# Moving half of the next step's level sums ahead of the mixing products, and the row transposes ahead of the B/C work, in a chunked scan

## Chip, cores, metric

One core of a Trainium2 chip runs the whole kernel in one launch. The metric is the device time of one execution in microseconds; the kernel before has a median of 4289.28 us in three runs (4289.17 to 4289.45).

## The reference, cut to what matters

The program is a small network on 2 sequences of 2048 tokens with 128 channels, float32: a block A (selective scan, time crystal, wavelet attention, mixture of experts, each behind a layer norm and a mask), then a top-4-head attention with 64 channels per head, an attention B, and the first attention once more. The change lies in the selective scan of block A alone:

```python
xz = x @ w_in                       # x: layer-normed tokens
xc, z = xz[..., :d_inner], xz[..., d_inner:]
xc = silu(causal_dwconv(xc, conv_w))
Bt, Ct = split(xc @ w_bc)
dt = softplus(xc * w_dt + dt_bias)
# per token t, channel c, state n
h   = exp(dt_t * A)[..., None] * h + (dt_t * xc_t)[..., None] * B_t[:, None, :]
y_t = einsum('bcn,bn->bc', h, C_t)
out = (y + d_skip * xc) * silu(z) @ w_out
```

## The kernel before

The scan (`phase_M`) takes 32 steps of 64 tokens of both sequences at once: 64 tokens of sequence 0 in partitions 0 to 63, those of sequence 1 in 64 to 127, 256 inner channels along the free axis. Within a step the recurrence is solved by levels: for distances of 1, 2, 4 and so on, decays are exponentials of partial sums of dt times A.

Each engine has its own function that lists its work in order (`pe`, `act`, `dve`, `pool`); signals (semaphores) tie them together, and an engine waits in that order. Of step i these matter:

- TensorE (`pe`): `pe_mix(i)` (L593, L595, L597), the mixing products, which wait for the weighed values of step i, its masked pairs, and y of step i-1. Then `pe_front(i + 1, j)`, j = 0 to 3 (L546 in steps 0 to 3, L549 later): the partial sums of the next step, four groups; with `pe_turn(i + 2)` (L557) between j = 1 and j = 2. Then `pe_bc(i + 2)` (L565, L569), `pe_y(i - 1)` (L604), `pe_pairs(i + 2)` (L577), in even steps `pe_out` (L613), then every eighth step `pe_t_ln` (L504) and `pe_t_out` (L515, L516, tanh products), and at the end the convolution of step i + 8 (`pe_conv`, L527 and L530), in step 0 four of them, in step 2 three, in step 1 and from step 24 on none. Before the convolutions 8, 16 and 24 (in steps 2, 8 and 16) stands `pe_ln` (L496), which turns the layer-normed rows of the next 512 tokens of each sequence into channels.
- ScalarE (`act`): the exponentials of the sums (`act_front`, L957 and L959), copies of `pe_turn` (L965), `pe_bc` (L972) and `pe_y` (L978); in the first step of each group of four absolute value and exponential of the new step sizes (`act_exps`, L940, L942), in the second the logarithm (`act_log`, L946); then `act_ln` (L902), the copies of the turned rows, where there are any, and the gate activation of the convolution (`act_silu`, L936), which writes m_xz. Every eighth step it has the root (L908) and the normed tokens of the time crystal (L916), or those of the scan (L896).
- VectorE (`dve`): `dve_skip`, `dve_mix` (L751 to L761, ending with y), `dve_raw` (L708, L709) for the convolution of the step before, then in the second step of a group `dve_rest` (L717, L719), in the third `dve_step_size` (L723, L724, L726), the masked pairs (L731), and the output.
- GpSimd (`pool`): `pool_front(i + 1)`, the weighing of the decays (L1076, three operations) and the skip product (L1080); then `pool_split(i + 2)` (L1062 to L1065), which cuts dt times A into three bfloat16 parts for `pe_front`, or, in the third step of a group, `pool_scale` (L1052, a split, L1055), which waits for `dve_step_size`.

PSUM banks 2 and 3 form a ring: the sums, the convolutions, the turned rows and the tanh products take them in turn, in a fixed list. Each use waits until the one two places ahead of it has been read by ScalarE:

```python
def pe_ring(*use):
    n = ring_at[use]
    if n >= 2:
        T.wait_ge(*ring_read[ring[n - 2][0]](*ring[n - 2][1:]))
    return ring_bank(*use)
```

The list has, per step i: the four sums of step i + 1, then tln or tc if any, then ln if any, then the convolution. `ring_read` is the exponential for a sum, and the gate activation for a convolution. Besides, `pe_front(i, 0)` waits for the split of step i from step 4 on.

Of the kernel before, what the change touches and what calls it, by code (L numbers as in the profile page):

```python
# [99 lines left out]
def build(nc, a, out, shape, phases=("M", "C", "D", "E", "F", "E2")):  # L100
# [5 lines left out]
    with ctx:  # L106
# [162 lines left out]
        def phase_M():  # L269
# [13 lines left out]
            with ExitStack() as st:  # L283
# [206 lines left out]
                def pe_ln(g):  # L490

                    T.wait_ge(*normed(g))
                    for b in bs:
                        bk = pe_ring("ln", g, b)
                        for q in range(4):
                            last = T.transpose(bank(bk)[:, q * P:(q + 1) * P], norm[:, 8 * (g % 2) + 4 * b + q, :], ident[:, :])  # L496
                        last.then_inc(*ln_turned.up(g, b))
# [54 lines left out]
                def pe_turn(i):  # L552
                    if i < Q4:
                        T.wait_ge(*silued(i))
                    bk = pe_misc("turn", i)
                    for c in range(C2):
                        last = T.transpose(bk[:, c * P:(c + 1) * P], xz[:, i % SLOTS, c * P:(c + 1) * P], ident[:, :])  # L557
                    last.then_inc(*x_turned.up(i))
# [22 lines left out]
                def pe_mix(i):  # L581

                    s, r = i % 2, i % 3
                    T.wait_ge(*val_done(i, 2))
                    T.wait_ge(*gm_done(i))
                    T.wait_ge(*state_done(-1))
                    if i:
                        T.wait_ge(*y_done(i - 1))
                    at = lambda b: dict(start=True, stop=True, skip_group_check=True, tile_position=(W * b, W * b))
                    slot = lambda l, b: bank(4 + l // 2)[half(b), (l % 2) * DI:(l % 2 + 1) * DI]  # L590
                    for l in range(LV):
                        for b in bs:
                            T.matmul(slot(l, b), gm[half(b), r, l, :], val[half(b), s, l, :], **at(b))  # L593
                    for b in bs:
                        T.matmul(slot(LV, b), bcs[half(b), r, 3 * N:4 * N], state[half(b), :], **at(b))  # L595
                    for b in bs:
                        last = T.matmul(slot(LV + 1, b), bcs[half(b), r, 0:N], val[half(b), s, SUF, :], **at(b))  # L597
                    last.then_inc(*mixed.up(i))
# [30 lines left out]
                def pe():  # L629
                    pe_ln(0)  # L630
                    T.wait_ge(*ld.all())
                    T.wait_ge(*tapped(0))
                    for k in range(Q4):
                        pe_conv(k)
                    for i in range(2):
                        pe_turn(i)
                        pe_bc(i)
                        pe_pairs(i)
                    pe_pool(0)
                    for j in range(4):  # L640
                        pe_front(0, j)
                    for i in ks:
                        pe_mix(i)
                        for j in range(4):
                            if i + 1 < SK:
                                pe_front(i + 1, j)
                            if j == 1 and i + 2 < SK:
                                pe_turn(i + 2)
                        if i + 2 < SK:
                            pe_bc(i + 2)  # L650
                        if i:
                            pe_y(i - 1)
                        if i + 2 < SK:
                            pe_pairs(i + 2)
                        if i == 0:
                            pe_pool(1)
                        if i == 1:
                            for b in bs:
                                pe_router(b)
                        if i % 2 == 0 and i:  # L660
                            pe_out(i // 2 - 1)
                        if i >= 10 and i % SLOTS == 2:
                            pe_t_ln(i // SLOTS - 1)
                        if i >= 10 and i % SLOTS == 3:
                            pe_t_out(i // SLOTS - 1)
                        for k in convs.get(i, ()):
                            if k % SLOTS == 0:
                                pe_ln(k // SLOTS)
                            pe_conv(k)
                    pe_y(SK - 1)  # L670
                    pe_out(NT - 1)
                    pe_t_ln(NG - 1)
                    pe_t_out(NG - 1)
                    leave(T)
# [224 lines left out]
                def act_ln(g):  # L899
                    for b in bs:  # L900
                        A.wait_ge(*ln_turned(g, b))
                        A.activation(chan(b, g), bank(ring_bank("ln", g, b)), ACT.Identity, bias=gain[:, 1:2],  # L902
                                     scale=gain[:, 0:1]).then_inc(*chan_done.up(g, b))
# [57 lines left out]
                def act_turn(i):  # L961
                    A.wait_ge(*x_turned(i))
                    if i >= 2:
                        A.wait_ge(*bc_made(i - 2))
                    A.copy(xT[:, i % 2], misc_bank("turn", i)[:, 0:C2 * P].rearrange("p (c t) -> p c t", c=C2)).then_inc(*xT_done.up(i))  # L965
# [19 lines left out]
                def act():  # L985
                    act_std("H", h_rs, 0)
                    act_std("M", n_rs, 0)
                    A.wait_ge(*ld.all())
                    act_ln(0)
                    act_std("H", h_rs, 1)  # L990
                    for k in range(Q4):
                        act_silu(k)
                    A.activation(neg_a[:, :], neg_a[:, :], ACT.Exp).then_inc(*exp_a.up(0))
                    act_exps(0)
                    for i in range(2):
                        act_turn(i)
                        act_bc(i)
                    act_log(0)
                    for j in range(4):
                        act_front(0, j)  # L1000
                    for i in ks:
                        q, at = i // Q4 + 1, i % Q4
                        for j in range(4):
                            if i + 1 < SK:
                                act_front(i + 1, j)
                            if j == 1 and i + 2 < SK:
                                act_turn(i + 2)
                        if i + 2 < SK:
                            act_bc(i + 2)
                        if i:  # L1010
                            act_y(i - 1)
                        if i == 1:
                            act_router()
                        if at == 0 and i and q < NQ:
                            act_exps(q)
                        if at == 1 and q < NQ:
                            act_log(q)
                        if i == 1 or (i % SLOTS == SLOTS - 1 and i // SLOTS + 2 < NG):
                            act_normed(i // SLOTS + (1 if i == 1 else 2))
                        if i >= 10 and i % SLOTS == 2:  # L1020
                            act_t_ln(i // SLOTS - 1)
                        if i >= 10 and i % SLOTS == 3:
                            act_tanh(i // SLOTS - 1)
                        for k in convs.get(i, ()):
                            if k % SLOTS == 0:
                                act_ln(k // SLOTS)
                            act_silu(k)
                        if i == 3:
                            A.wait_ge(*angle(0))
                            A.activation(cs[:, 0:1], tau[:, :], ACT.Sin)  # L1030
                            A.activation(cs[:, 1:2], th[:, :], ACT.Sin).then_inc(*sines.up(0))
                        if i >= 8 and i % SLOTS == 0:
                            act_t_std(i // SLOTS - 1)
                        if i >= 9 and i % SLOTS == 1:
                            act_t_normed(i // SLOTS - 1)
                        if i == 0:
                            act_std("M", n_rs, 1)
                            act_exps(1)
                    act_y(SK - 1)
                    act_t_std(NG - 1)  # L1040
                    act_t_normed(NG - 1)
                    act_t_ln(NG - 1)
                    act_tanh(NG - 1)
                    leave(A)
# [2103 lines left out]
```

## Time and profile before

| | |
|---|---|
| median of three runs | 4289.28 us |
| profiled execution | 4288.47 us |
| its span | 4287.2 us, 74987 instructions |
| TensorE busy (matmul) | 3584.7 us, 84% |
| VectorE busy | 3288.7 us, 77% |
| ScalarE busy | 2847.2 us, 66% |
| GpSimd busy | 1082.8 us, 25% |
| mean granted clock of TensorE | 0.827 |

The page cuts the span into 40 slices of 107 us; the scan's steps lie in the first five. The later slices belong to the other blocks. In the rows below, times are microseconds from the start of the span, a second number is a duration, and what stands in brackets at the end is how long the engine sat idle ahead of the instruction and what released it.

### The profile page before, as it was taken

The numbers are of one execution on the slowest core, as the hardware profiler recorded it, in microseconds if no ns is written. First come the engines' busy times: TensorE is split into PE (matmuls) and PEld (weight loads), VectorE is DVE, ScalarE is ACT, GpSimd is POOL, SyncE is SP. The second block draws the span as 40 slices with busy tenths as digits, with TensorE's granted clock in tenths as the row PEclk, the third lists the DMA queues.
The fourth block names the chain that finished last, engine by engine and source line by source line (L and its number), as shares of the span: only waits on it lengthen the run. The fifth ranks groups of instructions, "written<-read, shape, count | busy, mean of one in ns | idle before, by whom it ended". The sixth has DMA issues, their size and how long they took to land.

```text
span 4287.2 us, 74987 instructions
## 1 busy us (share of the span) xinstructions
PE 3584.7 (84%) x29132; PEld 1881.5 (44%) x29132; DVE 3288.7 (77%) x5099; ACT 2847.2 (66%) x4856; POOL 1082.8 (25%) x1610
## 2 busy tenths in 40 slices
PE   6888769998999998999998666666666668899999
PEld 4656512222444445676665122222122215566766
DVE  6888678886301137787888999999999987778887
ACT  3666426655434444666667999999999995566665
POOL 2666632100667630000000233322322210000000
PEclk8999859998999998999998555555555559999999
DMA  1000043320422110000000111011111010000000
GB/s 49 1 1 1 1 74 56 63 40 11 118 41 40 21 24 6 14 5 12 2 9 11 22 23 23 18 20 23 23 23 22 18 23 16 7 12 7 17 2 12
DMA packets 256883, 97.53 MB, mean 23 GB/s; under 512 B 223861, under 2 KB 241922, under 8 KB 256514
## 3 DMA queue, kind: packets, MB, share of 16 engines
q1 hardware_dynamic: 256530, 92.74, 10.9%
q8 instruction: 232, 3.80, 0.4%
q14 instruction: 121, 0.99, 0.1%
HBM read 31.75 MB, written 2.23 MB: 8 GB/s over the span
## 4 chain that ended last, share of the span: by engine, by line
PE 46%; DVE 32%; issue 12%; ACT 7%; POOL 1%; DMA 1%; SPq 1%; DVEq 0%; ACTq 0%; POOLq 0%
DVE d_negmax L2990 14%; PE psum L2540 7%; PE psum L2569 7%; DVE f_m_E L2645 6%; PE psum L2555 6%; PE psum L2223 5%; PE psum L2245 5%; ACT d_junk L3045 3%; PE psum L1501 2%; PE psum L1489 2%; DVE wl_negmax L1625 2%; DVE f_pT_E L2664 2%; PE psum L1478 2%; PE psum L593 1%; PE psum L527 1%
## 5 line engine op out<-in xcount | busy, mean ns | idle before, releaser
L2990 DVE TENSOR_REDUCE d_negmax<-psum 128x1 f32<-128x1024 f32 x1024 | 1170.8, 1210 | 8.5 <-PE psum L2930 6.4
L3045 ACT ACTIVATE d_junk<-psum,d_negmax 128x1024 bf16<-128x1024 f32 x1024 | 1136.8, 1127 | 29.7 <-DVE d_negmax L2990 25.3
L2930 PE MATMUL psum<-f_k,f_q_swapped 64*128 64x512 bf16 x2048 | 622.1, 604 | 420.0 <-ACT d_junk L3045 416.1
L2741 ACT ACTIVATE hidden<-psum,f_nm_E 128x1024 f32<-128x1024 f32 x512 | 566.5, 1113 | 146.6 <-DVE f_nm_E L2648 146.4
L2645 DVE TENSOR_REDUCE f_m_E<-psum 128x1 f32<-128x1024 f32 x512 | 601.9, 1216 | 50.8 <-PE psum L2540 49.5
L2540 PE MATMUL psum<-f_k,f_q_swapped 64*128 64x512 f32 x1024 | 527.3, 625 | 6.6 <-ACT hidden L2741 6.6
L2540 PE MATMUL psum<-f_k,f_q 64*128 64x512 f32 x1024 | 527.1, 625 | 2.9 <-DVE f_v_E L2636 1.9
L2748 ACT COPY f_pT_E<-psum 128x512 f32<-128x512 f32 x512 | 299.9, 586 | 321.2 <-PE psum L2555 321.2
L2569 PE MATMUL psum<-f_pT_E,f_v_E 128*64 128x128 f32 x8192 | 505.5, 276 | 2.5 <-DVE residual L2675 2.5
L2664 DVE COPY f_pT_E<-psum 128x512 f32<-128x512 f32 x512 | 351.3, 686 | 163.3 <-PE psum L2555 153.6
L2930 PEld LDWEIGHTS psum<-f_k,f_q_swapped 64*128 64x128 bf16 x2048 | 107.8, 101 | 830.4 <-ACT d_junk L3045 762.2
L2569 PEld LDWEIGHTS psum<-f_pT_E,f_v_E 128*64 128x64 f32 x8192 | 444.1, 137 | 20.0 <-ACT f_pT_E L2748 2.8
L2555 PEld LDWEIGHTS psum<-ident,hidden 64*128 64x128 f32 x8192 | 317.5, 140 | 242.9 <-issue 194.7
L2555 PE MATMUL psum<-ident,hidden 64*128 64x64 f32 x8192 | 358.5, 227 | 54.9 <-DVE f_pT_E L2664 50.8
L2357 POOL TENSOR_TENSOR moe_h<-moe_h,moe_gates_on_all 128x512 f32<-128x512 f32 x256 | 322.4, 1293 | 322.3 <-DMA moe_gates_on_all<-moe_gate_spill 188.9
L1766 ACT ACTIVATE wl_p<-psum 128x1024 f32<-128x1024 f32 x256 | 255.3, 1023 | 212.5 <-PE psum L1489 211.7
L1625 DVE TENSOR_REDUCE wl_negmax<-psum 128x1 f32<-128x1024 f32 x256 | 305.2, 1220 | 69.1 <-PE psum L1478 65.6
L2335 ACT ACTIVATE moe_h<-psum,moe_b 128x512 f32<-128x512 f32 x256 | 174.9, 688 | 254.7 <-PE psum L2245 254.7
L2223 PE MATMUL psum<-moe_h,moe_w 128*128 128x512 f32 x512 | 232.3, 597 | 3.4 <-POOL moe_h L2357 3.4
L3045 ACT ACTIVATION_READ_ACCUMULATOR d_junk<-psum,d_negmax 128x1 f32 x1024 | 214.9, 210 | 0.0
L2245 PE MATMUL psum<-normed_channels,moe_w 128*128 128x512 f32 x448 | 203.5, 597 | 4.3 <-DMA moe_w<-in_moe_w 4.3
L2540 PEld LDWEIGHTS psum<-f_k,f_q 64*128 64x128 f32 x1024 | 161.3, 189 | 92.6 <-ACT hidden L2741 78.4
(352 smaller groups left out, 4730.2 us busy)
## 6 DMA issues: line engine op xcount, KB each, us to landing
moe_gates_on_all<-moe_gate_spill SPq DMA_DIRECT2D x16, 1024.0 KB, 11.8
f_q_swapped<-f_q SPq DMA_DIRECT2D x64, 128.0 KB, 2.4
moe_w<-in_moe_w SPq DMA_DIRECT2D x15, 256.0 KB, 6.2
residual<-in_hidden_states SPq DMA_DIRECT2D x2, 768.0 KB, 7.9
out<-residual SPq DMA_DIRECT2D x1, 1024.0 KB, 7.3
wl_qT<-wl_q_rows SPq DMA_TRANSPOSE x48, 3.4
residual<-in_hidden_states SPq DMA_DIRECT2D x2, 256.0 KB, 3.2
m_taps<-in_m_conv SPq DMA_DIRECT2D x4, 128.0 KB
```

The costliest lines, as they stand in the source:

```text
L1625: V.tensor_reduce(negm[:, i, h:h + 1], two(slot("max", b, h, i)), X, ALU.max, negate=True).then_inc(*maxed.up(b, h, i))
L2223: last = T.matmul(acc, w2[:, e * FT + f, :], hbuf[:, n % 2, f, :], start=False, stop=(e == E_ - 1 and f == FT - 1))
L2245: T.matmul(bank(f), w1(e)[:, f * P:(f + 1) * P], chans[:, b, PAD + g * BANK:PAD + (g + 1) * BANK], start=True, stop=True).then_inc(*made.u ...
L2540: last = T.matmul(bank(2 * f + jj), (q if jj == h else q_sw)[half, w, qs], k2[half, w, h, f, :], start=True, stop=True)
L2555: last = T.transpose(bank(4 + r)[:, q * 64:(q + 1) * 64], pb[half, u % 2, kt * P:(kt + 1) * P], ident[half, half])
L2569: last = T.matmul(bank(6)[64 * h:64 * h + 64, 0:P], vt[:, n % 2, kt, h, :], pT[:, (2 * t + h) % 4, kt, :], start=(kt == 0), stop=(kt == NT ...
L2645: last = V.tensor_reduce(m2[:, u % 4, f:f + 1], two(2 * f), X, ALU.max)
L2664: V.tensor_copy(pT[:, u % 4, 8 * g:8 * g + 8, 64:P], bank(5).rearrange("p (q n) -> p q n", n=64)).then_inc(*pT_dve.up(u, g))
L2741: A.activation(pb[:, u % 2, f * 2 * BANK:(f + 1) * 2 * BANK], two(2 * f), ACT.Exp, bias=nm[:, u % 4:u % 4 + 1], scale=SC, accum_out=rs[:, ...
L2930: last = T.matmul(bank(2 + 2 * (at % 3) + jj), kT[half, s, jb * P:(jb + 1) * P], qT[half, s, hf * BANK:(hf + 1) * BANK], start=True, stop= ...
L2990: V.tensor_reduce(mh[:, t % 2, n // 2, n % 2:n % 2 + 1], two(2 + 2 * (at % 3)), X, ALU.max, negate=True).then_inc(*maxed.up(at))
L3045: A.activation(junk[:, at % 3, :], two(2 + 2 * (at % 3)), ACT.Exp, bias=mh[:, t % 2, n // 2, n % 2:n % 2 + 1], accum_out=sh[:, t % 2, n // ...
```

## The change

On TensorE, in steps i where i + 1 isn't a multiple of four (24 of the 31 steps that have a next one), `pe_front(i + 1, 0)` and `pe_front(i + 1, 1)` are issued ahead of `pe_mix(i)`; the others stay behind it. `pe_ln` moves from directly ahead of the convolution to directly behind the fronts, ahead of `pe_bc`. On ScalarE `act_ln` moves likewise, ahead of `act_bc`, and so ahead of `act_y` and `act_exps`. The ring's list stays as it is; so do all instructions of VectorE and GpSimd.

```diff
                     for i in ks:
+                        ahead = 2 if i + 1 < SK and (i + 1) % Q4 else 0
+                        for j in range(ahead):
+                            pe_front(i + 1, j)
                         pe_mix(i)
                         for j in range(4):
-                            if i + 1 < SK:
+                            if i + 1 < SK and j >= ahead:
                                 pe_front(i + 1, j)
                             if j == 1 and i + 2 < SK:
                                 pe_turn(i + 2)
+                        for k in convs.get(i, ()):
+                            if k % SLOTS == 0:
+                                pe_ln(k // SLOTS)
                         if i + 2 < SK:
                             pe_bc(i + 2)
...
                         for k in convs.get(i, ()):
-                            if k % SLOTS == 0:
-                                pe_ln(k // SLOTS)
                             pe_conv(k)
...
+                        for k in convs.get(i, ()):
+                            if k % SLOTS == 0:
+                                act_ln(k // SLOTS)
                         if i + 2 < SK:
                             act_bc(i + 2)
...
                         for k in convs.get(i, ()):
-                            if k % SLOTS == 0:
-                                act_ln(k // SLOTS)
                             act_silu(k)
```

## Rows read from the trace of the kernel before

**Rows 1.** Waits of TensorE, 57 to 517 us: total, times, longest.

```profile
PE psum L549 <- ACT m_decay L959: 19.3, 27, 4.3
PE psum L527 <- ACT normed_channels L902: 8.6, 3, 3.7
PE psum L549 <- ACT m_xz L936: 5.0, 5, 1.2
```

**Rows 2.** Timeline of TensorE, steps 3 to 7: start, duration, instruction, idle ahead.

```profile
128.71 1.48 PE L549 MATMUL psum<-m_dta_parts,level_sums_bf 128*128 128x256 bf16 x12
...
136.31 2.81 PE L593 MATMUL psum<-m_val,m_pairs 64*64 64x256 f32 x24
...
148.66 2.81 PE L593 MATMUL psum<-m_val,m_pairs 64*64 64x256 f32 x24
...
159.86 2.81 PE L593 MATMUL psum<-m_val,m_pairs 64*64 64x256 f32 x24
...
163.46 0.83 PE L549 MATMUL psum<-m_dta_parts,level_sums_bf 128*128 128x256 bf16 x6
165.14 0.83 PE L549 MATMUL psum<-m_dta_parts,level_sums_bf 128*128 128x256 bf16 x6 [0.85 <-ACT m_xz L936]
165.81 0.38 PE L557 MATMUL psum<-ident,m_xz 128*128 128x128 f32 x2
...
179.67 1.47 PE L549 MATMUL psum<-m_dta_parts,level_sums_bf 128*128 128x256 bf16 x12 [1.71 <-POOL m_dta_parts L1065]
```

**Rows 3.** Timeline of VectorE, steps 4 and 6, and line 723 (ns min/median/max).

```profile
140.32 1.23 DVE L751 TENSOR_TENSOR m_z<-psum,m_decay 128x1024 f32<-128x1024 f32 x1
...
146.49 0.83 DVE L709 TENSOR_TENSOR m_dtx<-m_dtx,m_dtb 128x256 f32<-128x256 f32 x1
...
164.07 1.22 DVE L751 TENSOR_TENSOR m_z<-psum,m_decay 128x1024 f32<-128x1024 f32 x1
...
172.19 1.75 DVE L723 TENSOR_TENSOR m_one_plus<-m_one_plus,m_dta 128x1024 f32<-128x1024 f32 x1
...
L723 DVE TENSOR_TENSOR m_one_plus<-m_one_plus,m_dta x8: 1226/2229/2840, 52.4 to 455.9; 128x1024 f32<-128x1024 f32 x8
```

**Rows 4.** Timeline of ScalarE, steps 4 and 5.

```profile
147.36 1.06 ACT L940 ACTIVATE m_dta<-m_dtx 128x1024 f32<-128x1024 f32 x1 [2.21 <-DVE m_dtx L709]
...
150.82 0.60 ACT L936 ACTIVATE m_xz<-psum 128x512 f32<-128x512 f32 x1
...
162.12 1.06 ACT L946 ACTIVATE m_one_plus<-m_one_plus 128x1024 f32<-128x1024 f32 x1 [3.32 <-DVE m_dta L719]
163.20 1.28 ACT L936 ACT_TABLE_LOAD   x1
164.49 0.60 ACT L936 ACTIVATE m_xz<-psum 128x512 f32<-128x512 f32 x1
```

**Rows 5.** Timeline of GpSimd, step 3: weighing of step 4, end of split 5.

```profile
130.70 4.28 POOL L1076 TENSOR_TENSOR m_val<-m_decay,m_dtx 128x768 f32<-128x768 f32 x3 [6.43 <-issue]
...
137.82 0.73 POOL L1065 TENSOR_TENSOR m_dta_parts<-m_dta_rest,m_dta_parts 128x256 bf16<-128x256 f32 x1
```

**Rows 6.** Timeline of TensorE: sums of step 20, mixings 20 and 31, sums of step 24.

```profile
359.83 1.48 PE L549 MATMUL psum<-m_dta_parts,level_sums_bf 128*128 128x256 bf16 x12
...
372.03 2.81 PE L593 MATMUL psum<-m_val,m_pairs 64*64 64x256 f32 x24
...
415.57 1.48 PE L549 MATMUL psum<-m_dta_parts,level_sums_bf 128*128 128x256 bf16 x12
...
506.53 2.81 PE L593 MATMUL psum<-m_val,m_pairs 64*64 64x256 f32 x24 [0.80 <-POOL m_val L1076]
```

**Rows 7.** Stretches of TensorE: length, busy (instructions), granted clock, DMA share, GB/s.

```profile
201.90:205.70 3.80, 3.77 (x20) 0.60 0.00 0
...
316.00:319.80 3.80, 0.11 (x3) 0.86 0.00 0
319.80:324.30 4.50, 4.50 (x22) 0.50 0.00 0
324.30:328.50 4.20, 4.20 (x34) 0.85 0.01 4
```

## Prediction

> **What bounds the kernel now.** I first read the page's slices: the scan (phase M) fills only the first 0.52 ms of 4287 us, and the change touches nothing outside it. Then I read who TensorE waits for inside the scan [rows 1]: 19.3 us in 27 waits of the sum products (L549) for the exponentials (L959), 8.6 us in three waits of the convolution products for the turned rows (L902), and 5.0 us in five waits for the gate activation m_xz (L936). These waits are what the change goes for. Then I followed steps 4 to 8 engine by engine. Names for the rest: E(i) is the end of the mixing products of step i, f0 to f3 of a step are its four sum groups (pe_front, j = 0 to 3), k is the convolution that a step issues last.
>
> TensorE carries most steps: the mixings of steps 4, 5 and 6 start at 136.31, 148.66 and 159.86 [rows 2], 12.35 and 11.20 us apart, and it waits little between. Mixing 6 runs 3.60 us (159.86 to 163.46). Beside that chain runs a second one, through three engines. After mixing 4 VectorE combines (L751, 140.32), weighs the newest tokens (L709, ends 147.32) [rows 3]; only then can ScalarE do its absolute value and exponential (L940, 147.36, after 2.21 us of waiting), load a table and run the gate activation of convolution 12 (150.82 to 151.42) [rows 4]. In step 5 it is the same with the logarithm: L946 waits 3.32 us, starts at 162.12, and activation 13 ends at 165.09 [rows 4]. In the kernel before, mixing 5 (148.66) and mixing 6 (159.86) are long under way when these activations end. That is the cover which I look at.
>
> **The change, part by part.** It removes and adds no operation. Part one moves f0 and f1 of step i+1 ahead of mixing i for 24 of the 31 steps that have a next one. Part two moves the row transposes (three times in the scan) and their copies ahead of the B/C work.
>
> *What f0 and f1 bring with them: two waits.* f0 waits for the three-part split of step i+1 by GpSimd. f1 waits for the bank that it writes: banks 2 and 3 alternate, a step uses five turns (four sums, one convolution), so f1 of step i+1 takes the bank of the convolution issued at the end of step i-1, and has to wait until ScalarE's gate activation has read it. The trace has this wait: f1 of step 7 starts at 165.14, 0.85 us idle, released by m_xz L936 [rows 2]; f0 had started at 163.46. Today mixing 6 stands ahead of that wait. After the change mixing 6 stands behind it, and behind mixing 6 the whole VectorE chain. TensorE doesn't pass a waiting product: in that row the transposes behind it (165.81) need nothing from ScalarE, and waited too.
>
> So in the first two steps of each group of four a loop closes: mixing i, combine, new tokens, exps or logarithm, gate activation, f1, mixing i+1. I add it from rows.
> - First step of a group: E(4) = 136.31 + 3.60 = 139.91, activation 12 ends at 151.42: 11.5 us. Plus 0.05 for the release, 0.66 for f1 (half of the 1.32 that twelve sum products take to the next start), 3.60 for the mixing: 15.8. VectorE began 0.4 us late there (140.32) [rows 3], so I take 15.6.
> - Second step: E(5) = 152.26, activation 13 ends at 165.09: 12.8, plus 4.3 is 17.1. GpSimd works less beside VectorE in a longer step, so 16.9.
> - Third step: f0 of the next group (step 8) starts at 179.67, after a wait for the split [rows 2]; VectorE had started mixing 6 at 164.07 [rows 3]: 15.6. VectorE's L723 took 1.75 us there; its fastest is 1.226 and its median 2.229 [rows 3], and the fast ones come where GpSimd is idle. In the new order GpSimd has finished its weighing by the time VectorE comes to L723, so I take 14.0 (13.3 to 15.6).
> - Last step: the next group's first f0 isn't moved. From f0 of step 4 (128.71) to the end of split 5 (137.82 + 0.73 = 138.55) it is 9.8 us [rows 2, 5]; then f0, f1 and the mixing, 1.32 + 3.60 + 0.05: 14.8. Mixing 4 itself needed nothing of split 5 and started at 136.31; its move behind f0 costs 2.3 us at once.
>
> A group is then 14.8 + 15.6 + 16.9 + 14.0 = 61.3 us. In two of five groups the tanh products stand in between: f0 of step 20 to mixing 20 is 12.2 us [rows 6], so the first term is 17.2, 2.4 more. Five groups: 306.5 + 4.8 = 311.3. Before, from f0 of step 4 (128.71) to f0 of step 24 (415.57), it was 286.9 [rows 2, 6]. **Plus 24.4 us.**
>
> *The clock.* Ten of these steps leave TensorE waiting for 3.3 to 6 us right ahead of f1 and the mixing (in step 4 its other work ends some 8 us after E(4), the release comes at 11.5). After 3.8 us of near idleness at 316.0 the granted clock was 0.50 for 4.5 us and 0.85 for the next 4.2; after the one ending at 201.9 it was 0.60 for 3.8 us, and then full but for a little [rows 7]. So the first lost 2.9 us, the second 1.6. f1 and mixing are only 4.3 us of work, so I take 1.6 for each: **plus 16 us** (0 to 28). The shorter waits ahead of f0 (2.3 us) I leave at nothing: after 1.71 us at 179.67 the products ran at full pace [rows 2].
> The Trainium skill's page "TensorE: Matmul & The Clock Gate", Part 1, says that the array's clock is halved after an idle stretch and comes back after sustained work; the trace agrees at 316.0 to 324.3. By it none of the ten waits would be free.
>
> *Table loads.* ScalarE's load stands inside both loops; it took 1.28 us at 163.20, and the activation followed 0.01 us behind it at 164.49 [rows 4].
> The Trainium skill, "ScalarE: Activation LUTs", section "What ACT_TABLE_LOAD costs", adds a drain of about 1.38 us to each switch. By that ten loops would be 14 us longer in all; the trace shows no such gap, and the measurement decides.
>
> *Steps 24 to 31* have no convolution, so f1 finds its bank free. What closes here: mixing i, f2 of step i+1, exponential, last weighing, skip product, split, f0, f1, mixing i+1. From the durations of step 4 (its weighing 4.28 us in three operations, 9.8 us from f0 to split) I estimate 11 to 12 us a step, 14 where ScalarE also has the layer norm's root. Eight mixings, the last ending at 506.53 + 3.60 = 510.1, took 94.6 us from 415.57 [rows 6]; I estimate 101. **Plus 6 us** (-1 to +12).
>
> *Part two and the saved waits.* In the old order the early rows would save two waits of 3.7 us and one of 1.2 [rows 1], and the half clock behind the two, 12 to 14 us. In the new order the convolution is no longer what is late there: its activation waits on ScalarE for the exps anyway. The 0.2 us that f2 waits for the exponential in a plain step goes too, but lies inside a step whose length is now set elsewhere. I credit 1 us, in step 2, whose mixing follows no such loop. Steps 0 to 3 otherwise even out.
>
> Sum: 24.4 + 16 + 6 - 1 = 45.4, taken as 45.5. The profiled execution took 4288.5 us, 0.8 under the median of 4289.3; with it 4334, against the median 4335.
>
> **The rivals.**
> 1. *The loops close, but the clock holds.* For it: waits of 1.7 us left the clock alone. Against it: both waits near 3.8 us didn't. With the low ends of the other terms (third step 13.3, steps 24 to 31 at -1) 4308, with the middle ones 4319.
> 2. *The saved waits win* (faster). Mechanism: the three early turnings and 24 saved waits of f2 (some 0.33 us each, 8 us) stay on the path, 20 us together: 4269. It needs the gate activation to be read before f0 has run, 0.7 us behind the convolution; it decides in steps 4, 5, 8, 9 and so on. The rows say that it is read 2.8 us (step 4: 151.42 against 148.66) and 5.2 us (165.09 against 159.86) after the convolution's end. In its favour is only that rows 1 show the waits it removes.
> 3. *They cancel*: the loops cost only the direct delay of each mixing, without carrying on into the next step, about half of 24, and part two returns 12: within 8 us of today.
> 4. *Worse*: half clock through the whole of each f1 and mixing and contended VectorE everywhere (group 63.4): 4360 and over.
>
> **How the numbers follow.** Forecast 0.60 (4319 to 4360); rival 1 0.20; rival 4 0.05; rival 3 0.08; rival 2 0.07. A measurement of this kernel tells about 0.2% (8.6 us) from no change. Slower by more: 0.85; within: 0.08; faster: 0.07. The range from 4308 (rival 1, low ends) to 4360 leaves out rivals 2, 3 and 4.
>
> **What would show it.** In the profile after: waits of L549 for m_xz L936 grow from 5.0 us to 35 us or more, ten of them over 3 us; mixings of steps 4, 5 and 6 lie 15.5 to 19 us apart; waits of the convolution for L902 vanish; f2's waits for L959 almost vanish; the scan ends some 45 us later, everything after it keeps its length. Wrong if mixings stay 11 to 12 us apart, or if waits for m_xz are few.

## The result

The kernel after takes 4332.81 us, the median of three runs (4328.47 to 4336.06), against 4289.28 us before: 1.0099 times as long, with a 95% interval of 1.0081 to 1.0117. It is slower by 43.5 us; the forecast was 4335, in a range of 4319 to 4360. The profiled execution took 4328.47 us, 40.0 more than that of before.

From the page of after: the span, the busy times that answer to the table of before, and two rows of its 40 slices (108 us each) in tenths, TensorE's busy share and its granted clock:

```profile
span 4327.2 us, 74987 instructions
...
PE 3598.8 (83%) x29132; PEld 1886.0 (44%) x29132; DVE 3262.2 (75%) x5099; ACT 2852.5 (66%) x4856; POOL 1062.1 (25%) x1610
...
PE   6888859999899998999998666666666659899999
...
PEclk8999968999999999999999555555555559899999
```

As many instructions as before. TensorE is busy 14 us longer and VectorE 26 us shorter, while the span is 40 us longer. So neither engine got much more work; what grew is idle time.

The waits of TensorE in the scan, in the order total, times, longest, from 57 to 570 us (line numbers after the change lie 3 to 5 higher: L936 is now L940, L1065 is L1070, L959 is L963):

```profile
PE psum L549 <- ACT m_xz L940: 35.0, 11, 4.7
PE psum L549 <- POOL m_dta_parts L1070: 34.4, 19, 5.0
...
PE psum L549 <- ACT m_decay L963: 1.1, 5, 0.2
```

Against [rows 1]: the waits that the change goes for are gone. Those of the sums for the exponentials fell from 19.3 to 1.1 us, and none of the convolution for the turned rows is left. In their place stand 35.0 us for the gate activation, which were 5.0, and 34.4 us in 19 for GpSimd's split, which were 6.1 in 4.

Steps 4 to 7 after, on TensorE (start, duration, instruction, idle time ahead and its releaser):

```profile
127.44 1.48 PE L549 MATMUL psum<-m_dta_parts,level_sums_bf 128*128 128x256 bf16 x12
...
137.42 1.47 PE L549 MATMUL psum<-m_dta_parts,level_sums_bf 128*128 128x256 bf16 x12 [2.31 <-POOL m_dta_parts L1070]
138.82 2.81 PE L593 MATMUL psum<-m_val,m_pairs 64*64 64x256 f32 x24
...
153.38 1.33 PE L549 MATMUL psum<-m_dta_parts,level_sums_bf 128*128 128x256 bf16 x6 [3.02 <-ACT m_xz L940]
154.64 3.94 PE L593 MATMUL psum<-m_val,m_pairs 64*64 64x256 f32 x24
...
171.09 1.46 PE L549 MATMUL psum<-m_dta_parts,level_sums_bf 128*128 128x256 bf16 x6 [4.70 <-ACT m_xz L940]
172.48 3.55 PE L593 MATMUL psum<-m_val,m_pairs 64*64 64x256 f32 x24
...
190.22 1.90 PE L549 MATMUL psum<-m_dta_parts,level_sums_bf 128*128 128x256 bf16 x12 [2.62 <-POOL m_dta_parts L1070]
```

and on ScalarE and VectorE, for [rows 3, 4]:

```profile
149.26 1.06 ACT L944 ACTIVATE m_dta<-m_dtx 128x1024 f32<-128x1024 f32 x1 [3.25 <-DVE m_dtx L713]
...
152.72 0.60 ACT L940 ACTIVATE m_xz<-psum 128x512 f32<-128x512 f32 x1
...
159.56 1.23 DVE L755 TENSOR_TENSOR m_z<-psum,m_decay 128x1024 f32<-128x1024 f32 x1 [7.57 <-PE psum L597]
...
168.07 1.06 ACT L950 ACTIVATE m_one_plus<-m_one_plus 128x1024 f32<-128x1024 f32 x1 [3.81 <-DVE m_dta L723]
...
170.44 0.60 ACT L940 ACTIVATE m_xz<-psum 128x512 f32<-128x512 f32 x1
...
177.02 1.23 DVE L755 TENSOR_TENSOR m_z<-psum,m_decay 128x1024 f32<-128x1024 f32 x1 [7.52 <-PE psum L597]
```

In before mixings 4, 5 and 6 lay 12.35 and 11.20 us apart [rows 2]; here mixings 5 and 6 lie 17.8 us apart. Read the rows in a circle. The gate activation ends at 153.32; f1 starts at 153.38, and mixing 5 behind it at 154.64. Its last product lets VectorE go at 159.56, after 7.57 us without work. VectorE's work lets ScalarE take the logarithm at 168.07, the activation behind it ends at 171.04, and f1 starts at 171.09. So the circle is f1, mixing, VectorE, ScalarE, f1, and every engine in it waits for the one before it. VectorE's waits for the mixing's last product grew from 66.1 us in 18 to 143.1 us in 24 (57 to 570 us).

For the runs below I take one mark as the scan's end, the transposes of its last y, here before and after:

```profile
515.91 0.69 PE L604 MATMUL psum<-ident,m_y 128*128 128x128 f32 x2 [5.34 <-DVE m_y L761]
```

```profile
562.79 0.69 PE L604 MATMUL psum<-ident,m_y 128*128 128x128 f32 x2 [5.33 <-DVE m_y L765]
```

The scan is longer by 46.9 us.

### The profile page after: what moved, and what is told of

The parts are those of the page before. It is cut to its first block, busy times and chain, and to the rows that moved or that the text cites. A ratio compares the mean times of both kernels' runs of the same rounds, so it can differ in the third digit from the quotient of the medians.

```text
span 4327.2 us, 74987 instructions
## 1 busy us (share of the span) xinstructions
PE 3598.8 (83%) x29132; PEld 1886.0 (44%) x29132; DVE 3262.2 (75%) x5099; ACT 2852.5 (66%) x4856; POOL 1062.1 (25%) x1610
## 3 DMA queue, kind: packets, MB, share of 16 engines
q1 hardware_dynamic: 256530, 92.74, 10.7%
## 4 chain that ended last, share of the span: by engine, by line
PE 40%; DVE 29%; issue 12%; ACT 6%; DMA 1%; SPq 0%; POOL 0%; DVEq 0%; ACTq 0%; POOLq 0%
DVE d_negmax L2995 14%; PE psum L2545 7%; PE psum L2574 6%; DVE f_m_E L2650 6%; PE psum L2560 6%; PE psum L2228 5%; PE psum L2250 5%; ACT d_junk L3050 3%; PE psum L1506 2%; PE psum L1494 2%; DVE wl_negmax L1630 2%; DVE f_pT_E L2669 2%; PE psum L1483 2%; ACT wl_p L1771 1%; DVE residual L2680 1%
```

## The experiments

All diffs are against the kernel after. "Scan end" is the start of the product just shown. Before ran beside them at 4288.3 to 4290.3 us.

| kernel | scan end | median us | to before [95%] |
|---|---|---|---|
| before | 515.9 | 4289.28 | |
| after | 562.8 | 4332.81 | 1.0099 [1.0081, 1.0117] |
| ln_only | 509.2 | 4276.76 | 0.9967 [0.9954, 0.9979] |
| fronts_only | 581.5 | 4349.01 | 1.0132 [1.0115, 1.0149] |
| one_ahead | 530.5 | 4302.77 | 1.0027 [1.0016, 1.0038] |
| silu_first | 530.9 | 4301.31 | 1.0027 [1.0017, 1.0036] |
| split_first | 552.2 | 4328.62 | 1.0099 [1.0082, 1.0116] |
| both_first | 519.8 | 4294.03 | 1.0010 [1.0001, 1.0020] |
| both_none_ahead | 508.2 | 4276.66 | 0.9977 [0.9968, 0.9987] |
| fill | 573.7 | 4348.95 | 1.0147 [1.0130, 1.0164] |
| fill_half | 549.5 | 4322.70 | 1.0079 [1.0062, 1.0096] |
| only_0 | 522.9 | 4291.50 | 1.0009 [1.0000, 1.0019] |
| only_1 | 526.5 | 4295.34 | 1.0016 [1.0006, 1.0026] |
| only_2 | 533.2 | 4308.22 | 1.0046 [1.0029, 1.0063] |

### The two parts apart

ln_only is part two alone, one line of TensorE's list:

```diff
-                        ahead = 2 if i + 1 < SK and (i + 1) % Q4 else 0
+                        ahead = 0
```

> Part two alone: the turned rows go early, no sum group goes ahead of the mixing. The last y transpose of the scan starts at 515.9 us before and at 562.8 after the change. Theory (the loop through the gate activation costs the time, part two is sound by itself): the waits of 3.7, 3.7 and 1.2 us for L902 go, and with them the half clock behind two of them, so the scan ends 10 to 14 us before 515.9, and the kernel takes 4275 to 4279. Rival (part two harms too, because the copies now stand ahead of those of B/C and y on ScalarE): 4289 or more.

It is the fastest kernel of the study together with both_none_ahead below: 4276.76 us (4275.96 to 4279.37), 12.5 under before. The scan ends at 509.2, 6.8 earlier and not 10 to 14. Its two long waits did go. Ahead of the convolution of step 8 stood 3.69 us for the copies; mixing 8 to mixing 9 was 187.25 to 205.73 in before and is 186.17 to 199.87 now, 18.5 against 13.7 us. The second such place gives 5.4 us. Three of these ten microseconds are lost again at step 11 (mixing 11 to 12 took 15.8 us, now 18.8), by the clock. The granted clock over 243.2 to 250.3 is 0.52 (stretch: length, busy, clock, DMA share, GB/s), where the same products in before, the second row, had 1.00:

```profile
243.20:250.30 7.10, 7.10 (x31) 0.52 0.00 0
```

```profile
249.50:253.58 4.08, 4.08 (x30) 1.00 0.00 0
```

By the medians the kernel gains 5.7 us more than its scan, by the two profiled executions 2.3 us more (4288.47 against 4279.37). Where it gains them was not found; the last section comes back to it.

fronts_only is part one alone: `pe_ln` and `act_ln` back where they were in before.

```diff
-                        for k in convs.get(i, ()):
-                            if k % SLOTS == 0:
-                                pe_ln(k // SLOTS)
                         if i + 2 < SK:
                             pe_bc(i + 2)
...
                         for k in convs.get(i, ()):
+                            if k % SLOTS == 0:
+                                pe_ln(k // SLOTS)
                             pe_conv(k)
```

> Part one alone: two sum groups ahead of the mixing, the rows turned late as before. Theory: in steps 8 and 16 the copies of the turned rows now wait behind the exps on ScalarE, the convolution behind the copies and its gate activation behind that, all inside the loop that ends in f1; so this is 7 to 9 us longer than the whole change, scan end near 571, kernel near 4341. Rival (the convolution is off the path in the new order, part two worth nothing): scan end 562 to 564.

The sign is as expected, the size isn't: the scan ends at 581.5, so part two is worth 18.7 us inside the new order, not about 8.

```profile
PE psum L549 <- ACT m_xz L939: 33.0, 10, 4.7
PE psum L549 <- POOL m_dta_parts L1068: 32.0, 19, 5.7
...
PE psum L527 <- ACT normed_channels L905: 10.7, 3, 4.7
```

(L939, L1068 and L905 stand here for L940, L1070 and L906 of after.)

The three waits of the convolution are back, and are longer (10.7 us). In this order they cost more than their own length: the convolution's activation is what f1 of the next step but one waits for, so a late convolution delays the next mixing too. From mixing 8 to mixing 9 and from 16 to 17 it took 20.4 and 20.5 us, against 15.3 in the kernel after. That makes 10.3 of the 18.7 us; 3.9 us more are there by mixing 8 (206.40 against 202.55), and the rest was not placed.

### Which of the moved groups

one_ahead moves f0 only. f1, which needs the convolution's bank, stays behind the mixing.

```diff
-                        ahead = 2 if i + 1 < SK and (i + 1) % Q4 else 0
+                        ahead = 1 if i + 1 < SK and (i + 1) % Q4 else 0
```

> The whole change, but only f0 goes ahead of the mixing. f0 waits only for the split and for a bank whose reader is long done; f1, the group with the wait for the gate activation, stays behind. Theory: the ten waits of L549 for m_xz ahead of a mixing vanish, mixings of steps 4 to 7 lie 11 to 13 us apart again, scan end 505 to 518, kernel within 12 us of before. Rival (any sum group ahead of the mixing does it, through the split and the lower clock): scan end above 540.

Between the two: 530.5. All waits for m_xz are gone, and 32 of the 47 us with them, so the bank is the main cause. But it leaves 14.6 us over before, and more than 21 over ln_only. They sit at the other signal:

```profile
PE psum L549 <- POOL m_dta_parts L1070: 45.3, 18, 4.1
```

f0 waits for a split that GpSimd finishes only after weighing, and now a mixing waits behind f0. My forecast priced it in the first step of each group, at the first f0 of the next group, and in steps 24 to 31. Here it also stands ahead of mixings 6, 10, 14, 18 and 22, 3.19 us each time.

### The two late producers

silu_first takes the cause away at ScalarE: the gate activation is issued ahead of the exponential, the logarithm and the normed tokens, none of which the convolution needs. (`act_t_ln` and `act_tanh` of the time crystal, which stood right ahead of it, move up with it; the lines below don't show them.)

```diff
-                        if at == 0 and i and q < NQ:
-                            act_exps(q)
-                        if at == 1 and q < NQ:
-                            act_log(q)
...
                         for k in convs.get(i, ()):
                             act_silu(k)
+                        if at == 0 and i and q < NQ:
+                            act_exps(q)
+                        if at == 1 and q < NQ:
+                            act_log(q)
```

> The whole change, and ScalarE does the gate activation ahead of exps and logarithm (and of the normed rows) instead of behind them. Nothing else differs. Theory: the bank of the convolution is read 0.7 us after its end, so f1 waits under 0.5 us; the loop is broken; mixings 11 to 13.5 us apart, scan end 505 to 525. What is left are the waits for the split. Rival (the loop closes through the exponential or the split anyway): scan end above 545.

530.9: 32 of 47 us come back, as with one_ahead, by another way. The activation of step 4 now starts at 149.44, right behind the convolution, and f0, f1 and mixing 5 follow one another at full pace:

```profile
149.33 1.59 PE L549 MATMUL psum<-m_dta_parts,level_sums_bf 128*128 128x256 bf16 x12
150.85 2.81 PE L593 MATMUL psum<-m_val,m_pairs 64*64 64x256 f32 x24
```

Mixing 5 starts at 150.85 and mixing 6 at 163.30, 12.5 us apart, where the kernel after has 17.8. What is left is the split:

```profile
PE psum L549 <- POOL m_dta_parts L1070: 40.7, 19, 5.0
```

split_first takes that away instead: GpSimd splits step i+2 ahead of weighing step i+1.

```diff
                     for i in ks:
+                        if i + 2 < SK and i % Q4 != 2 and i + 2 > Q4:
+                            pool_split(i + 2)
                         if i + 1 < SK:
                             pool_front(i + 1)
                         if i % Q4 == 2 and i // Q4 + 1 < NQ:
                             pool_scale(i // Q4 + 1)
-                        elif i + 2 < SK and i % Q4 != 2 and i + 2 > Q4:
-                            pool_split(i + 2)
```

> The whole change, and GpSimd splits step i+2 ahead of weighing step i+1 instead of behind it; ScalarE's order as in the change. The scan's last y transpose starts at 562.8 us after the change, 530.9 with the gate activation first, 509.2 with part two alone. Theory: of the 34 us that f0 waits for the split most go, but in the groups up to step 23 they lie beside the loop through the gate activation except in the first step of a group and steps 24 to 31, so the scan ends 10 to 18 us earlier, at 545 to 553, and the waits of f1 for m_xz stay at 35 us or rise. Rival (the split's waits are the main cost): scan end below 535.

552.2, as expected. The split waits fall from 34.4 to 10.3 us, and the waits for m_xz grow from 35.0 to 39.3: while the circle through ScalarE is closed, an earlier f0 mostly waits longer at f1.

```profile
PE psum L549 <- ACT m_xz L940: 39.3, 12, 4.7
PE psum L549 <- POOL m_dta_parts L1070: 10.3, 5, 2.6
```

both_first has both edits.

> The whole change with both: gate activation ahead of exps and logarithm, split ahead of the weighing. Theory: both waits that came with the change are gone, scan end 503 to 515, kernel 4275 to 4287. Rival (something else in the new order costs, as VectorE starting its combination later): scan end above 522.

519.8, outside the 503 to 515 that I gave. All but freed of both producers (4.8 us in 3 are left for m_xz, 8.9 in 5 for the split), the early sums still don't pay. The sums f2 wait again for the exponentials, 19.3 us in 14, as much as in before, and the waits of the mixing for the last y are 8.4 us in 2, where after had 2.3 in 1:

```profile
PE psum L549 <- ACT m_decay L963: 19.3, 14, 3.6
PE psum L549 <- POOL m_dta_parts L1070: 8.9, 5, 2.6
PE psum L593 <- DVE m_y L765: 8.4, 2, 6.1
```

both_none_ahead tells what the order of sums and mixing is worth once both producers are early: it is both_first with `ahead = 0`.

> Part two, gate activation first and split first, but no sum group ahead of the mixing. It tells what the early sums bring once their waits are gone. Theory: scan end 500 to 509, the gate activation's waits of L549 (5.0 us) gone; the early sums are worth 5 us at most either way. Rival (early sums pay once freed): both_first ends its scan over 6 us before this one.

508.2, as expected, and 4276.66 us (4268.98 to 4285.65 in ten runs). The early sums cost 11.6 us of the scan even here. Of these, 2.9 us are there by mixing 4 (138.08 against 135.22), nearly nothing is added up to mixing 12 (251.06 against 247.95), and 3.8 us come behind mixing 24 (420.17 against 412.39). What costs them was not tested. Against ln_only the two freed producers bring 1.0 us of the scan and nothing in the time (0.9977 and 0.9967, intervals overlapping). They are worth something only where sums go early.

### The clock

The stretch behind the wait of step 5, f1 and mixing 5 of the kernel after, had a granted clock of 0.67, and that behind the wait of step 6 had 0.71:

```profile
153.38:158.60 5.22, 5.22 (x32) 0.67 0.02 3
...
171.09:176.10 5.01, 5.01 (x34) 0.71 0.01 3
```

fill puts products into ten of the waits ahead of f1: those of the mixing once more, into the banks that the mixing overwrites next. They need nothing that is new and nobody reads them. The first try took too many of them, 12 to 38.

```diff
+                fill = {5: 24, 6: 38, 9: 12, 10: 32, 13: 24, 14: 38, 17: 12, 18: 32, 21: 24, 22: 38}
...
                         for j in range(ahead):
+                            if j == 1 and i in fill:
+                                pe_fill(i, fill[i])
                             pe_front(i + 1, j)
```

> The whole change, with extra products between f0 and f1 in the ten steps where f1 waits for the gate activation: 12 to 38 of the mixing's own products, about as long as the wait (1.3 to 4.2 us), written where the mixing writes right after. TensorE then isn't idle there. Theory (idleness ahead of f1 costs half clock in f1 and the mixing, 14 us by the longer durations in the trace): the L593 groups of steps 5, 6, 10, 13, 14, 18, 21, 22 go from 3.5 to 5.1 us back to 2.8, and the scan ends 8 to 14 us earlier, at 549 to 555. Rival (the clock isn't on the path): scan end 560 to 565.

The filling of step 5 took 5.40 us for a wait of 3.02, so the mixing came later by more than the clock gave back: 573.7. It is no measure of the clock's price; it shows only that the mixings are back at 2.81 us.

```profile
150.92 5.40 PE L609 MATMUL psum<-m_val,m_pairs 64*64 64x256 f32 x48
...
157.01 2.81 PE L593 MATMUL psum<-m_val,m_pairs 64*64 64x256 f32 x24
```

fill_half has about half as many, 4 to 18 products (each is two instructions in the trace; `fill = {5: 12, 6: 18, 9: 4, 10: 14, 13: 12, 14: 18, 17: 4, 18: 14, 21: 12, 22: 18}`).

> As fill, with about half as many extra products (4 to 18 products, two array instructions each), since in fill they ran 5.4 us where f1 waited 3.0, and held f1 back. Now they should end just before the gate activation. Theory (half clock in f1 and the mixing is on the path): mixings of steps 5, 6, 10, 13, 14, 18, 21, 22 take 2.8 us in the L593 group, f1 0.8, and the scan's last y transpose starts at 548 to 555, against 562.8 after the change. Rival (clock not on the path): 560 to 565.

This one fits: in step 5 the filling leaves 0.29 us of waiting, and all waits for m_xz together are 5.7 us.

```profile
150.19 2.81 PE L609 MATMUL psum<-m_val,m_pairs 64*64 64x256 f32 x24
...
153.28 0.83 PE L549 MATMUL psum<-m_dta_parts,level_sums_bf 128*128 128x256 bf16 x6 [0.29 <-ACT m_xz L956]
154.04 2.81 PE L593 MATMUL psum<-m_val,m_pairs 64*64 64x256 f32 x24
```

```profile
153.28:157.60 4.32, 4.32 (x38) 1.00 0.00 0
```

With more work on TensorE the scan ends at 549.5, 13.3 us earlier than after. In one place, mixing 5, it is 154.64 + 3.94 against 154.04 + 2.81, 1.7 us. But not all of the 13.3 us lies behind the ten waits. From mixing 4 to 7, 8 to 11, 12 to 15, 16 to 19 and 20 to 23, where the fillings stand, fill_half gains 3.0, 1.9, 2.9, 1.3 and 3.2 us, 12.3 together. Between mixings 11 and 12, where none stands, it gains 3.5 (21.63 us in after, 18.15 here), because after ran the last tanh products and the convolution there at a clock of 0.60 (262.0 to 270.5), and this kernel at 1.00 (255.9 to 262.0). And behind mixing 24 it loses 2.5 again, with mixings 30 and 31 at 5.38 and 4.50 us. So the clock behind the ten waits costs some 12 us. It isn't the same for each: in after, seven of the ten waits are followed by a mixing of 3.55 to 5.05 us, and three, of 1.68, 3.03 and 1.69 us, by one of 2.81. Two waits of the same length differ (steps 13 and 21):

```profile
285.09 0.83 PE L549 MATMUL psum<-m_dta_parts,level_sums_bf 128*128 128x256 bf16 x6 [3.03 <-ACT m_xz L940]
285.85 2.81 PE L593 MATMUL psum<-m_val,m_pairs 64*64 64x256 f32 x24
...
412.31 0.88 PE L549 MATMUL psum<-m_dta_parts,level_sums_bf 128*128 128x256 bf16 x6 [3.02 <-ACT m_xz L940]
413.12 4.40 PE L593 MATMUL psum<-m_val,m_pairs 64*64 64x256 f32 x24
```

### Which step of the group

only_0, only_1 and only_2 move f0 and f1 in one of the three steps of each group alone (i % 4 = 0, 1, 2):

```diff
-                        ahead = 2 if i + 1 < SK and (i + 1) % Q4 else 0
+                        ahead = 2 if i + 1 < SK and i % Q4 == 0 else 0
```

> Part two, and f0 and f1 ahead of the mixing only in the first step of each group of four (8 steps), where the early group waits for the split, and not for exps or logarithm. Base is part two alone, scan end 509.2. Theory: steps 4, 8, 16 and 24 lose the split's 2.3 us and some clock, scan end 517 to 524. Rival (early sums are harmless here): 507 to 512.

> The same, only in the second step of each group: mixings 5, 9, 13, 17, 21 now stand behind the gate activation that follows the exps. Theory: each loses 3 to 4 us and some clock, what follows doesn't loop, scan end 524 to 534. Rival (one step alone is absorbed by the slack of the next): 509 to 515.

> The same, only in the third step of each group: mixings 6, 10, 14, 18, 22 stand behind the gate activation that follows the logarithm, and VectorE's step sizes for the next group behind that mixing. Theory: VectorE starts 5 to 7 us later in these steps, of which 1 to 2 us is slack in the split of the next group; scan end 529 to 540. Rival (absorbed): 509 to 515. The three together should make up the 53.6 us between part two alone and the whole change.

All three fall in their ranges: 522.9, 526.5 and 533.2. Over ln_only (509.2) that is 13.7, 17.3 and 24.0 us, in sum 55.0, and all together cost 53.6. The costs add up, but this doesn't show that the steps leave each other alone, for the waits are not those of the kernel after. ln_only has 7.1 us in 6 for the split and 5.0 in 5 for m_xz. With i % 4 = 0 f0 waits 17.0 us in 9 for the split; with 1 f1 waits 11.4 us in 10 for m_xz, and f0 13.7 in 8 for the split. The dearest, 2, falls in its range by another wait than I named: for m_xz it waits 4.5 us in 5, less than ln_only, and for the split 40.0:

```profile
PE psum L549 <- POOL m_dta_parts L1070: 40.0, 14, 5.8
```

## Why the prediction was right

The likeliest case came, near the middle of its range. By its own steps:

- **The circle through ScalarE.** Foretold were 35 us or more of waits for m_xz, ten of them over 3 us, and mixings of steps 4 to 6 lying 15.5 to 19 us apart. There are 35.0 us in 11, eight of them over 3 us, and the mixings start at 138.82, 154.64 and 172.48, 15.8 and 17.8 us apart. silu_first, which takes this cause away at ScalarE, and one_ahead, which takes only f1 out of it, end within 0.4 us of each other, 32 us earlier than after. That is shown.
- **A group's length.** From f0 of step 4 to f0 of step 24 I had 311.3 + 16 = 327.3 us; it is 127.44 to 449.39, 322.0. The third step was 13.2 us and not 14.0 (VectorE's start at 177.02 to f0 at 190.22, and 13.2 in the four other groups too): 4 us over five groups. The lower end that I had given was 13.3. VectorE's L723 [rows 3], L727 now, shows it: in its seven later instances the median was 2.29 us and is 1.22, which had been the fastest. That it's GpSimd, done earlier, which leaves VectorE its pace fits with this (in before it worked beside L723 at 227.86, which took 2.84 us; in after it stands idle from 180.59 to 185.82, around L727 at 183.26), but was not tested apart. Before and after (ns, min/median/max):

```profile
L723 DVE TENSOR_TENSOR m_one_plus<-m_one_plus,m_dta x7: 1536/2285/2840, 113.9 to 455.9; 128x1024 f32<-128x1024 f32 x7
```

```profile
L727 DVE TENSOR_TENSOR m_one_plus<-m_one_plus,m_dta x7: 1215/1220/1682, 115.2 to 499.3; 128x1024 f32<-128x1024 f32 x7
```

- **The clock.** 16 us forecast for ten waits, some 12 measured by fill_half in the steps that it fills. Rival 1, that it holds, falls: 0.67 and 0.71 were granted. But the prediction's "none of the ten waits would be free" is not so: they were 1.68 to 4.70 us long and not 3.3 to 6, and three were free. That the waits of 2.3 us at f0 cost nothing held in step 4 (1.47 us at 137.42), not everywhere: at 190.22, after 2.62 us, the products took 1.90.
- **Steps 24 to 31.** The term that was mis-sized: +6 us (-1 to +12) forecast; from f0 of step 24 to the scan's mark it was 100.3 us (415.57 to 515.91) and is 113.4 (449.39 to 562.79), +13.1. I had put the circle at 11 to 12 us a step, and from mixing 24 (460.88) to mixing 31 (551.74) it is 13.0 on average. Part of it is clock, which I hadn't counted here: f0 waits up to 5.01 us, and the stretch from that wait on had a clock of 0.66.

```profile
486.03 2.72 PE L549 MATMUL psum<-m_dta_parts,level_sums_bf 128*128 128x256 bf16 x12 [5.01 <-POOL m_dta_parts L1070]
488.68 4.17 PE L593 MATMUL psum<-m_val,m_pairs 64*64 64x256 f32 x24
```

```profile
486.00:494.00 8.00, 7.97 (x47) 0.66 0.00 0
```

  Four mixings of these steps run over 2.81 us (3.44, 4.17, 3.17, 4.28), 3.8 us in all, and three pairs of f0 and f1 over 1.48 (2.47, 2.72, 2.72), 3.5 us. Before has slow ones there too (a mixing of 4.43 us in step 26, 1.6 us), so in these products the clock makes some 5.7 us of the 13.1. The other products were not added up.
- **Part two.** 1 us credited, and f0 of step 4 does start 1.3 us earlier (127.44 against 128.71); against fronts_only part two is worth 18.7. I had said that the convolution isn't what is late in the new order. It is, in the steps where it waits for the turned rows. The sum isn't touched by it, since I took the steps with the turned rows as plain ones. On its own I had given it 12 to 14 us in the old order, and it measured 6.8.
- **The split.** The signs that I gave name only m_xz, and the split's waits are as long, 34.4 us in 19. In the sum they were not forgotten: 5.9 us stand ahead of mixings 4, 8 and 16, 10.3 at the first f0 of a group, 15.1 in steps 24 to 31, and for each of these the sum has a term. Only 3.1 us stand ahead of mixings 6, 10, 14, 18 and 22, where f1 behind them waits longer for m_xz. What the split costs is 10.6 us of the 47 by split_first, and 11 with the circle open (530.9 against 519.8).
- **Rival 2** (the saved waits win) asked for activations read at once. both_first comes near that, and still ends 11.6 us behind the same kernel with the sums in their old place. The waits for exponentials that this rival saves are not saved there: they are 19.3 us again.

The errors (5 us too much in the groups, 7 too little behind them) cancel: 46.9 us of scan measured, 45.5 forecast. That the sum comes so near is in part luck; the mechanism isn't. The time itself rose by less, 40.0 us between the profiled executions, since later stages gave some back. One place of it: in the attention of block A, behind a wait of 2.37 us that both kernels have (ahead of 1009.20 and of 1055.85), before ran at a clock of 0.61 over 1011.0 to 1024.8, and after at 1.00 in the same products:

```profile
1011.07 1.90 PE L1501 MATMUL psum<-wl_p,wl_v 128*9 128x512 f32 x8
...
1024.78 1.05 PE L1501 MATMUL psum<-wl_p,wl_v 128*9 128x512 f32 x8
```

```profile
1056.85 1.05 PE L1506 MATMUL psum<-wl_p,wl_v 128*9 128x512 f32 x8
...
1066.15 1.05 PE L1506 MATMUL psum<-wl_p,wl_v 128*9 128x512 f32 x8
```

These are the first and the fifth of the same groups of products. Between them the offset of the two kernels shrinks from 45.8 us (1056.85 - 1011.07) to 41.4 (1066.15 - 1024.78). The other 2.5 us were not placed.

## What to carry to other kernels

An engine works through its list in order, so moving work ahead of a critical instruction moves that work's waits ahead of it too. List what the moved work waits for, a bank taken in turns included, and see when each signal comes; if one of them hangs on the instruction that was passed, the move closes a circle. The length of a wait in the list isn't what its removal brings: 18 us of waits for exponentials went with the change and longer ones came in their place, while one move of three row transposes (ln_only), for 8.6 us of waits, took 12.5 us off the kernel.

## What the runs showed of the hardware

- The clock of a stage far behind the edit differs between the traces of two kernels: 0.61 in before and 1.00 in after, some 500 us behind the scan. Whether the edit did it isn't shown, for one and the same kernel, before, ran between 4281.2 and 4295.9 us over nineteen runs. ln_only gained 12.5 us in time for 6.8 us in the scan. Between kernels whose scans differ by less than some 5 us this is more than the difference; the scan's mark tells them apart better than the time does. Whether the clock makes all of that scatter wasn't tested.
- A clock dip needs no long wait directly in front of it: ln_only had 0.52 over 7.1 busy microseconds (243.2 to 250.3), where before had none in the same products, and in the 9 us ahead of it TensorE waited 0.21 us at most. Nor does a wait of about 3 us always bring one: behind 3.03 us the clock was 1.00 (285.0 to 290.0), behind 3.02 us it was 0.68 (412.2 to 417.5). What sets the moment stays open.
- Products that nobody needs can be cheaper than waiting: 10 fillings made the scan 13.3 us shorter. They have to fit: with twice as many it became 10.9 us longer.
- The Trainium skill, "TensorE: Matmul & The Clock Gate", Part 1, says for modelling that the penalty of the ramp is under 1% of a typical kernel. What the clock costs in the whole of this kernel wasn't measured. The ten waits' part of it is under 1%, some 12 of 4333 us, but it is a quarter of the 46.9 us by which the change lengthened the scan.
